# A cross-attention kernel on one core: the out projection's contraction packed into three groups of 128 rows, and the loop over batches written out

## The reference

```python
q = heads(hidden_states @ W_q)
k_t, v_t = heads(text_ehs @ W_k), heads(text_ehs @ W_v)
probs_t = softmax(einsum('bhsd,bhtd->bhst', q, k_t) * attn_scale)
text_out = einsum('bhst,bhtd->bhsd', probs_t, v_t)
k_ip, v_ip = heads(ip_ehs @ W_k_ip), heads(ip_ehs @ W_v_ip)
attn_scores = einsum('bhsd,bhnd->bhsn', q, k_ip) * attn_scale
qsem = l2norm(einsum('bhst,bte->bhse', probs_t, text_ehs))
sem = einsum('bhse,bne->bhsn', qsem, l2norm(ip_ehs))
probs_ip = softmax(attn_scores + 0.5 * sem) * spatial_mask[None, None, :, None]
ip_out = einsum('bhsn,bhnd->bhsd', probs_ip, v_ip)
out = (text_out + ip_out) @ W_out + b_out + residual
```

## Time and profile before

| | |
|---|---|
| median of 3 runs | 360.89 us (360.53 to 361.3) |
| the profiled execution: its time, its span | 363.37 us, 361.6 us |
| busy: PE, DVE, ACT, POOL | 332.5, 304.6, 299.9, 165.0 us |
| instructions: PE, DVE, ACT, POOL | 2434, 2068, 1303, 314 |
| mean granted TensorE clock | 0.995 |
| chain that ended last: PE, ACT, DVE, issue, DMA | 68%, 13%, 11%, 5%, 2% |
| moved by DMA | 16.72 MB, mean 46 GB/s |

### The profile page before, as it was taken

The page is one execution under the profiler, slowest core; times in us unless marked ns, Lnnn a source line. Parts: engine busy times, 40 slices in busy tenths (PEclk is TensorE's granted clock), DMA queues, the critical chain, the costliest instruction groups (busy, mean ns, idle before and its releaser), DMA issues.

```text
span 361.6 us, 10181 instructions
## 1 busy us (share of the span) xinstructions
PE 332.5 (92%) x2434; PEld 312.3 (86%) x2434; DVE 304.6 (84%) x2068; ACT 299.9 (83%) x1303; POOL 165.0 (46%) x314
## 2 busy tenths in 40 slices
PE   4799998889999999989999999979999999999974
PEld 4797877778999999989999999979999999999863
DVE  5557567999999999977999999979999999999963
ACT  4646699989899999977989999979999999999941
POOL 2034602636464646463464646444646464524241
PEclk9999999999999999998999999999999999999999
DMA  6940011000101010101001010101010101000001
GB/s 230 327 130 0 2 45 49 2 1 21 56 20 56 21 55 22 55 25 44 29 24 38 31 39 18 56 23 54 20 54 19 55 19 54 20 21 18 20 20 54
DMA packets 14301, 16.72 MB, mean 46 GB/s; under 512 B 1928, under 2 KB 13704, under 8 KB 14248
## 3 DMA queue, kind: packets, MB, share of 16 engines
q1 hardware_dynamic: 14248, 16.20, 14.4%
HBM read 10.13 MB, written 5.24 MB: 43 GB/s over the span
## 4 chain that ended last, share of the span: by engine, by line
PE 68%; ACT 13%; DVE 11%; issue 5%; DMA 2%; SPq 1%; ACTq 0%
PE gv_ps L936 18%; PE mi_ps L963 14%; PE mi_ps L899 11%; PE et_ps L923 9%; PE sc_ps L915 8%; ACT e_sb L554 7%; DVE place_ctxT L709 2%; DMA x_nat<-in_x 2%; DVE qs L691 2%; ACT qs L546 2%; PE mi_ps L881 2%; PE gv_ps L1054 1%; DVE negmax L701 1%; PE mi_ps L950 1%; DVE u_all L840 1%
## 5 line engine op out<-in xcount | busy, mean ns | idle before, releaser
L554 ACT ACTIVATE e_sb<-sc_ps,negmax 128x60 f32<-128x60 f32 x640 | 146.7, 315 | 15.5 <-DVE negmax L701 13.5
L936 PE MATMUL gv_ps<-tab,place_w 128*128 128x162 f32 x640 | 115.4, 302 | 3.2 <-ACT place_ctxT L563 3.0
L709 DVE CUSTOM_DVE_ANT_0 place_ctxT<-gv_ps,e_sb 128x60 f32<-128x60 f32 x640 | 99.7, 211 | 11.9 <-PE gv_ps L936 11.3
L936 PEld LDWEIGHTS gv_ps<-tab,place_w 128*128 128x128 f32 x640 | 94.7, 191 | 4.4 <-issue 4.3
L915 PE MATMUL sc_ps<-km,qs 128*128 128x256 f32 x320 | 77.5, 324 | 0.2 <-DVE qs L691 0.2
L492 POOL TENSOR_TENSOR place_w<-place_ctxT,rsum 128x320 f32<-128x320 f32 x32 | 23.8, 745 | 116.9 <-DVE rsum L819 116.9
L923 PE MATMUL et_ps<-ident,e_sb 128*128 128x128 f32 x320 | 64.5, 283 | 10.2 <-ACT e_sb L554 9.4
L701 DVE TENSOR_REDUCE negmax<-sc_ps 128x4 f32<-128x240 f32 x160 | 63.4, 396 | 0.0
L567 ACT COPY place_w<-et_ps 128x256 f32<-128x256 f32 x160 | 62.3, 389 | 0.7 <-PE et_ps L923 0.7
L923 PEld LDWEIGHTS et_ps<-ident,e_sb 128*128 128x128 f32 x320 | 39.1, 140 | 21.3 <-ACT e_sb L554 15.9
L709 DVE DVE_READ_ACCUMULATOR2_ANT quad<- 128x1 f32 x640 | 52.5, 82 | 0.0
(11 more groups left out here) (153 smaller groups left out, 587.6 us busy)
## 6 DMA issues: line engine op xcount, KB each, us to landing
x_nat<-in_x SPq DMA_DIRECT2D x16, 320.0 KB, 3.1
out<-place_w SPq DMA_DIRECT2D x32, 160.0 KB, 1.8
place_ctx<-in_ctx SPq DMA_DIRECT2D x4, 256.0 KB, 3.4
place_w<-in_L_xattn_W_v SPq DMA_DIRECT2D x1, 640.0 KB, 8.5
place_w<-in_L_xattn_W_k SPq DMA_DIRECT2D x1, 640.0 KB, 10.2
place_w<-in_L_xattn_W_k_ip SPq DMA_DIRECT2D x1, 640.0 KB, 11.7
place_w<-in_L_xattn_W_v_ip SPq DMA_DIRECT2D x1, 640.0 KB, 9.9
place_ctxT<-place_w SPq DMA_DIRECT2D x16, 40.0 KB, 1.9
```

What stands on the lines that cost most here:

```text
L554: last = nc.scalar.activation(e_sb[:, slot, TOK * j:TOK * j + T], sc_ps[:, bank, TOK * j:TOK * j + T], ACT.Exp, bias=negmax[:, slot, j:j + 1])
L709: last = v.tensor_tensor_reduce(out=junk[:, u % 2, j, 0:T], in0=gv_ps[:, u % 2, TABW * j:TABW * j + T], in1=e_sb[:, u % ERING, TOK * j:TOK ...
L936: last = mm(gv_ps[:, u % 2, 2 * TABW * r:2 * TABW * r + 2 * TABW], eT[:, u % TRING, P * r:P * r + P], tab[:, batch.parity, h:h + 2, :].rea ...
```

## The change

- The four image tokens' weights of a head sum to the mask (softmax, then times the mask). So three of them, and the mask, say as much as four: the contraction becomes 320 rows of attention + 60 rows (20 heads x 3, for the differences of v_ip to the last token's) + 1 row of the mask (for the last token's v_ip, summed over the heads) + 1 row of ones (for the bias) = 382 rows, which are padded to three groups of 128. A tile is gathered in `mixed`, transposed by three transposes and projected by nine products; the third group's right side is `u_all`, now 126 rows: the last 64 rows of W_out, 60 of u, one of the last token, the bias.
- ACT's three copies of the transposed tile become one of 384 columns, and so do DVE's three subtractions.
- Part 0 of the out projection has five products instead of six, part 1 four instead of five.
- GpSimd no longer adds the bias to x; its load and buffer are gone. `mixed` keeps four tiles.
- At the start DVE makes the differences of the image tokens (`ip_dif`, two operations) and gathers the last token's values (`vip_last`, three small copies). The five blocks of u have 96 rows, and there is a sixth of 8 rows, three products that are accumulated, with a sixth copy. PE, ACT and SP wait for six blocks. Only two thirds of W_out are split into `wo_parts`.
- SP places u by 34 transfers: 16 of 24 rows, 8 of 12 rows, 8 of one row, one that spreads the last 64 rows of W_out to all eight batches, one for the bias. ACT waits for all 34 before its first copy of u_all, in the same unit as before.
- The last tile: two transposes and six products, then one transpose and three products.
- All 8 batches are written out, with constants in the waits.

The diff, cut to that:

```diff
-        wo_parts = sb("wo_parts", [P, 2, QC, C], F32R)
-        bias_all = sb("bias_all", [P, C])
+        wo_parts = sb("wo_parts", [P, 2, 2, C], F32R)
...
-            sp.wait_ge(u_copied, 5)
+            sp.wait_ge(u_copied, 6)
+            sp.dma_start(u_nat[0:64], w_out[2 * P:C, :].unsqueeze(1).to_broadcast([64, B, C])).then_inc(u_placed, DMA)
             for b in range(B):
                 for m in range(2):
-                    r, blk = 32 * (b % 4), 2 * m + b // 4
-                    sp.dma_start(u_nat[32 * m:32 * m + 32, b], u_sb[r:r + 32, blk]).then_inc(u_placed, DMA)
-                sp.dma_start(u_nat[64:80, b], u_sb[16 * b:16 * b + 16, 4]).then_inc(u_placed, DMA)
+                    r, blk = 24 * (b % 4), 2 * m + b // 4
+                    sp.dma_start(u_nat[64 + 24 * m:88 + 24 * m, b], u_sb[r:r + 24, blk]).then_inc(u_placed, DMA)
+                sp.dma_start(u_nat[112:124, b], u_sb[12 * b:12 * b + 12, 4]).then_inc(u_placed, DMA)
+                sp.dma_start(u_nat[124:125, b], u_sb[b:b + 1, 5]).then_inc(u_placed, DMA)
+            sp.dma_start(u_nat[125:126], b_out.rearrange("(a b c) -> a b c", a=1, b=1).to_broadcast([1, B, C])).then_inc(u_placed, DMA)
...
-                    nc.scalar.copy(attnT[:, 0:2 * P], ps[:, 0:2 * P])
-                    nc.scalar.copy(attnT[0:64, 2 * P:3 * P], ps[0:64, 2 * P:3 * P])
-                    nc.scalar.copy(attnT[0:IPROWS, 3 * P:4 * P], ps[0:IPROWS, 3 * P:4 * P]).then_inc(attnT_hi, 1)
+                    nc.scalar.copy(attnT[:], mi_ps[:, misc_bank(("at", 0, index)), 0:QC * P]).then_inc(attnT_hi, 1)
...
                     if u == U_SLOT:
-                        act.wait_ge(u_placed, 3 * B * DMA)
-                    nc.scalar.copy(u_all[0:IPROWS, u - U_SLOT, 0], u_nat[0:IPROWS, u - U_SLOT]).then_inc(u_hi_made, 1)
+                        act.wait_ge(u_placed, U_PLACED * DMA)
+                    nc.scalar.copy(u_all[0:OUT_ROWS, u - U_SLOT, 0], u_nat[0:OUT_ROWS, u - U_SLOT]).then_inc(u_hi_made, 1)
...
+                v.tensor_tensor(attnT_low[:], mi_ps[:, misc_bank(("at", 0, t)), 0:QC * P], attnT[:].bitcast(F32),
+                                ALU.subtract).then_inc(attnT_lo, 1)
...
                 for c in range(QC):
-                    tr(ps[0:QROWS[c], P * c:P * c + P], attn[:, par, P * c:P * c + QROWS[c]], ident[:])
-                tr(ps[0:IPROWS, 3 * P:4 * P], pip[:, par].rearrange("p h n -> p (h n)"), ident[:]).then_inc(attnT_done, 1)
+                    last = tr(ps[:, P * c:P * c + P], mixed[:, t % ARING, P * c:P * c + P], ident[:])
+                last.then_inc(attnT_done, 1)
...
+                steps = [(high[:, P * c:P * c + P], wo_parts[:, n, c, :]) for c in range(2) for n in range(2)]
+                steps += [(low[:, P * c:P * c + P], wo_parts[:, 0, c, :]) for c in range(2)]
+                high2, low2 = high[0:OUT_ROWS, 2 * P:3 * P], low[0:OUT_ROWS, 2 * P:3 * P]
+                steps += [(high2, u_all[0:OUT_ROWS, b, 0, :]), (high2, u_all[0:OUT_ROWS, b, 1, :]),
+                          (low2, u_all[0:OUT_ROWS, b, 0, :])]
...
+            pe.wait_ge(u_copied, 3)
+            for m in range(QC):
+                last = mm(BANKS[U_BANKS[5]][0:B, 0:C], vip_last[0:QROWS[m], m, :], wo[0:QROWS[m], m, :],
+                          start=m == 0, stop=m == QC - 1)
+            last.then_inc(pre_u, 1)
+            pe.wait_ge(u_copied, 6)
...
-            with eng.Fori(0, LOOP_STEPS) as step:
-                for place in range(2):
-                    body(Batch(step=step, place=place))
...
+            for u in range(ALL_UNITS + 2 * GROUPS - 2):
```

More of the change, by code:

```diff
@@ L351, in store @@
[L351 to L363, removed]
@@ L454, in _ @@
                 pool.wait_ge(k_lo, 2 * c + 2)
-                km_step(Batch(0), c)
-            pool.wait_ge(in_bias, DMA)
+                km_step(0, c)
             pool.wait_ge(in_mask, DMA)
-            add_bias(Batch(0), 0)
-            def nxt(batch):
-                return (Batch(batch.number + 1) if batch.step is None else
-                        Batch(step=batch.step, place=batch.place + 1))
-            def builds(batch, s, part):
-                if not batch.has(1, 1, B):
+            g.tensor_copy(mixed[:, :, MASK_COL:MASK_COL + 1], mask_sb[:].unsqueeze(2)).then_inc(consts_made, 1)
@@ L528, in _ @@
+            for t in range(ALL_TILES + 2):
+                tile(t)
         @block.scalar
@@ L669, in _ @@
+            for u in range(ALL_UNITS + GROUPS + 1):
+                slot(u)
+            act.wait_ge(last_done, 1)
+            nc.scalar.copy(last_attnT[:, 0:2 * P], LAST_ATTN[:, 0:2 * P]).then_inc(last_hi, 1)
+            act.wait_ge(last_done, 2)
+            nc.scalar.copy(last_attnT[:, 2 * P:3 * P], LAST_IP).then_inc(last_hi, 1)
         @block.vector
@@ L672, in _, with x_low @@
             v.memset(tab[:], 0.0).then_inc(zeros_made, 1)
-            for place in range(YRING):
-                dve.sem_inc(y_stored[place], DMA)
-            def x_low(batch, half, n):
-                dve.wait_ge(xT_hi, batch.count(2 * HALVES, 2 * half + n + 1))
-                ps = mi_ps[:, misc_bank(batch, half - 1, "x", n), :]
+            def x_low(half, n):
+                dve.wait_ge(xT_hi, 2 * half + n + 1)
+                ps = mi_ps[:, misc_bank(("x", n, half)), :]
                 if n == 0:
@@ new lines, in add_residual, with slot @@
+            def add_residual(product, t):
+                dve.wait_ge(out_done, t + 1)
+                if t >= YRING:
+                    dve.wait_ge(y_stored[t % YRING], DMA * (t // YRING))
+                v.tensor_tensor(y_sb[:, t % YRING], product, x_nat[:, t // 2 % XRING, t % 2], ALU.add).then_inc(y_made, 1)
+            def slot(u):
+                t, j = divmod(u, GROUPS)
+                before, before2 = 0 <= t - 1 < ALL_TILES, 0 <= t - 2 < ALL_TILES
+                par, par2 = (t - 1) % 2, t % 2
+                if u + LEAD < ALL_UNITS:
+                    maxima(u + LEAD)
@@ L1133 @@
+                if not early and u < ALL_UNITS:
+                    table_products(u)
+            for u in range(ALL_UNITS + 2 * GROUPS - 2):
+                if u == ALL_UNITS + GROUPS + 1:
+                    last_attn_transposes()
+                slot(u)
+            last_products()
 _INS = ["x", "ctx_2048", "fside_S_0", "L0_xattn_W_q", "L0_xattn_W_k", "L0_xattn_W_v",
```

665 lines of the change are left out of this document (282 added, 383 removed).

## The result

The changed kernel took 351.85 us (median of 5 runs, the kernel before beside it 360.53); the ratio is 0.973, with a 95% interval of 0.970 to 0.976. In a second measurement it took 350.91 against 361.15, ratio 0.9734 (0.9705 to 0.9764). So it is 2.7% faster, 8.7 to 10.2 us. The forecast was 349.6, between 344.5 and 358.

What follows compares the result with a forecast made beforehand. PE was taken to set the pace, DVE and ACT right behind. -8.8 - 0.84 - 5.5 - 1.9 + 1.6 + 4.1 = -11.3 us took the profiled 363.4 to 352.1; less 2.5, 349.6 us, range 344.5 to 358.

Steps and rivals of the forecast that it cites:

- The steady half: Each half batch (two tiles) gets 0.63 us shorter, bounds 0.30 to 1.0; over fourteen halves -8.8 us.
- the wait of 0.18 for DVE's low halves: PE's wait before six out-projection products goes as DVE finishes 0.44 earlier, but only 0.04 of it counts.
- so PE sets the pace: In the steady half PE, 92% busy, bounds the kernel, with DVE (84%) and ACT (83%) right behind.
- Rival B: DVE and ACT take the gain: the half shrinks by 0.3 only, 354.2 us; chance 0.10.
- ACT's saving: One copy of 384 columns of the transposed tile in place of three saves ACT 0.17 us a tile.
- The loop: Written-out batches lose the stops after two jumps: 3.55 (some 1.6 of it half clock) and 1.93, sum -5.5 us.
- The 2.5: The old kernel's runs had median 360.9, 2.5 under the profiled 363.4; the same was taken off 352.1.
- The stop: In unit 10 ACT waits for SP to place u: 3.3 plus 0.8 for half clock, +4.1 us (1 to 6).
- over 6 us: Sign of being wrong: ACT's wait before its first u_all copy is over 6 us; about 3 expected.
- rival A: Small transfers placing u cost SP 0.29 more for each of 24 issues; stall grows by 7.0, 356.6 us; chance 0.14.
- DVE's 0.84 in the second half of batch 0: That half is DVE's, so two tiles' shorter subtractions count nearly whole: 2 x 0.42, -0.84 us.
- Rivals C and D: C: SP's issues queue behind the w_out load, 367.1, chance 0.07; D: straight code stalls as the loop did, 355.1, chance 0.04.

Runs made afterwards that it cites:

- exp. 2: The kernel before with only its batches (and SP's loop) written out: 356.83 us, ratio 0.9895 to the kernel before.
- exp. 6: The changed kernel with only DVE's subtraction in three pieces again: 364.06 us, ratio 1.0059 to the kernel before.
- exp. 7: The changed kernel with only ACT's copy in three pieces again: 358.81 us, ratio 0.9922 to the kernel before.
- exp. 4: The changed kernel with ACT's copy and DVE's subtraction both in three pieces again: 365.88 us, ratio 1.014 to the kernel before.
- exp. 5: The changed kernel with PE's eleven products and four transposes a tile put back, some done twice: 358.65 us, ratio 0.9918 to the kernel before.
- exp. 12: The changed kernel with U_SLOT 14, and DVE's guard and image softmax reciprocal left out: 344.85 us, ratio 0.9565 to the kernel before.
- exp. 10: The kernel before with u's transfers cut to 24 and 12 rows, number unchanged, a quarter of u's rows unplaced: 360.79 us, single execution.
- exp. 3: The changed kernel with the first unit that needs the placed u moved from 10 to 14 (U_SLOT): 345.55 us, ratio 0.9564 to the kernel before.
- exp. 8: The changed kernel with U_SLOT 14, u's sixth block made in unit 7 and its rows placed last: 344.79 us, ratio 0.9534 to the kernel before.
- exp. 11: The changed kernel with U_SLOT 14, and the guard's square made on GpSimd by plain multiplication: 344.5 us, ratio 0.9552 to the kernel before.
- exp. 9: The changed kernel with U_SLOT 14, and both reciprocals moved from DVE to GpSimd as a power of -1: 465.69 us, ratio 1.2899.

## Why the prediction was right, and where its steps were not

**The steady half.** Forecast -0.63, bounds 0.30 to 1.0. The stretches above give -0.80; over all whole halves, the two with a jump and the one behind the first left out, the mean goes from 18.63 to 17.86, -0.77. Between the marks that makes 10.7 us (16.2 less 3.9 for the jumps and 1.6 for a clock, below) where the forecast had 8.8. The bound of 17.7 to 18.35 held. The part of the chain that shrank is the out projection:

```profile
192.34 0.73 PE mi_ps L865 x5
...
194.09 0.59 PE mi_ps L865 x4
...
200.68 0.74 PE mi_ps L865 x5
...
202.53 0.59 PE mi_ps L865 x4
```

These are 2.65 a half. Before, the pieces at the same places were 0.89 and 1.07 and, between them, two of five products:

```profile
186.21 0.74 PE mi_ps L963 x5
...
196.01 0.73 PE mi_ps L963 x5
```

together 3.43. Of the 0.78 less, 0.59 are the four products, whole as forecast. The rest is the wait of 0.18 for DVE's low halves: it went whole, where I counted 0.04. This is the term that was mis-sized. The transposes, counted at nothing, gave nothing: the 0.11 that the chain no longer spends on one of them comes back at the scores two steps later.

The step "so PE sets the pace" was only half of the mechanism, and the price of 0.04 for DVE came from it. The half periods tell it:

| kernel | PE | DVE | ACT | half, us |
|---|---|---|---|---|
| before | as before | as before | as before | 18.65 |
| exp. 2 | as before | as before | as before | 18.60 |
| changed | less | less | less | 17.85 |
| exp. 6 | less | as before | less | 18.61 |
| exp. 7 | less | less | more than before | 18.29 |
| exp. 4 | less | as before | more than before | 18.68 |
| exp. 5 | as before | less | less | 18.33 |
| exp. 12 | less | still less | less | 17.87 |

Against exp. 2, which is written out like the changed kernel, PE's saving and ACT's without DVE's give nothing (exp. 6), the shorter copies without PE's saving 0.27 (exp. 5), all together 0.75. So before there were two paths of nearly the same length, and the longer, by some 0.3, was not PE's alone but the one that passes through DVE: the stretch of the chain shown in exp. 6 runs over its subtractions. Rival B saw that risk, but gave it to the wrong side: DVE did not take the gain, it made it possible. GpSimd's saving is in all these runs but exp. 2, and in exp. 6 it gives nothing either.

**ACT's saving: sized about right, and not tested.** The forecast had 0.17 a tile. The groups by line look as if it were 0.43, since the means of the three copies are 398, 271 and 274 ns and that of the one is 517:

```profile
L629 ACT CAST attnT<-mi_ps 128x256 fp32r<-128x256 f32 x31 | 12.3, 398 | 2.0 <-PE mi_ps L951 2.0
...
L631 ACT CAST attnT<-mi_ps 80x128 fp32r<-80x128 f32 x31 | 8.5, 274 | 0.0
L630 ACT CAST attnT<-mi_ps 64x128 fp32r<-64x128 f32 x31 | 8.4, 271 | 0.0
```

But these lengths overlap. In order of time, in the kernel before, each copy starts before the one ahead of it has ended:

```profile
332.58 0.37 ACT L629 CAST attnT<-mi_ps 128x256 fp32r<-128x256 f32 x1
...
332.85 0.26 ACT L630 CAST attnT<-mi_ps 64x128 fp32r<-64x128 f32 x1
...
333.01 0.27 ACT L631 CAST attnT<-mi_ps 80x128 fp32r<-80x128 f32 x1
```

The three take 0.70 from first start to last end and the one takes 0.52: 0.18 less. In exp. 7 the third piece lies in other rows (64 to 127), and it starts only when the second has ended, as does the operation behind it:

```profile
147.44 0.40 ACT L549 CAST attnT<-mi_ps 128x256 fp32r<-128x256 f32 x1
147.70 0.30 ACT L550 CAST attnT<-mi_ps 64x128 fp32r<-64x128 f32 x1
148.01 0.26 ACT L551 CAST attnT<-mi_ps 64x128 fp32r<-64x128 f32 x1
148.36 0.92 ACT L473 ACTIVATE e_sb<-sc_ps,negmax 128x60 f32<-128x60 f32 x4
```

From the first start to the start of the next operation, where ACT didn't wait, the medians are 0.58 before, 0.37 in the changed kernel and 0.84 in exp. 7. So exps. 4 and 7 put 0.47 a tile on ACT where the change had taken 0.21 off. Exp. 7's 0.44 a half is the price of that, and an upper bound for ACT's own saving; what this is worth alone isn't shown. Why the pieces of exp. 7 don't overlap stays open. On DVE the pieces of exp. 6 cost what they did before (0.95 and 0.94, by the same measure). DVE's forecast was exact, 0.55 for 384 columns against 0.553.

**The loop.** Forecast -5.5; exp. 2 measured -3.8, and exp. 10's two stretches with a jump give (20.61 - 18.65) + (20.58 - 18.65) = 3.9. The other 1.6 was the half clock after the first jump, which that profiled execution had and exp. 10's had not. The 2.5 by which the profiled execution was above the median can be taken apart with exp. 10, which has the loop and ran at the median (360.79). The profiled one had this 1.6 more, and a start 1.6 longer, where the first x arrived late; exp. 10 had a slower end, by 0.7. The chains at the same place of the start, before and in exp. 10:

```profile
3.57 7.17 DMA x_nat<-in_x
...
39.74 1.95 PE mi_ps L1034 x12
```

```profile
38.16 1.96 PE mi_ps L1034 x12
```

I let the change take the clock's 1.6 away and then took it off once more inside the 2.5. That step failed: without it the forecast would have been 351.2, between the two measured medians (350.91 and 351.85). The late start was rightly taken off.

**The end.** Forecast -1.9, measured 14.98 - 16.97 = -2.0.

**The start and the stop.** The block's products take 1.82 on the chain where I had 1.6. The stop costs 5.4 (exp. 3) against a forecast of 4.1 with bounds of 1 to 6. ACT's wait in it is 6.2 where I had 3.8, and "over 6 us" was one of my own signs of being wrong: it came true, though the time stayed in the range. Sized too small were two terms. SP's 34 issues took from 46.06 to 70.73, 24.7 us or 0.73 each, where I had 22.1 and 0.65: rival A's mechanism was there at less than half its price, some 0.12 instead of 0.29 for each of the 24, or 2.9 us. Exp. 10 shows it in the old kernel by the number of rows alone. The rule of the Trainium skill ("DMA: Bandwidth & Descriptors", on why a DMA increments its semaphore by 16) agrees with these rows: 24 and 12 rows divide over 12 engines, not 16, and the sequencer that issues has the missing increments to write. The eight issues of a single row were cheaper (0.54 to 0.56), which took back some 0.4. And the clock fell to 0.50 for 3.9 us, as after the first jump and not as after the second, so the full price was due and not half of it. The Trainium skill's statement ("TensorE: Matmul & The Clock Gate", Part 1), that an idle PE falls to half clock, agrees with this stop; in exp. 10 PE was idle for about 1.8 us at each jump, in two pieces, and the clock stayed at 1.00. ACT came to the wait at 66.1 and not 67.2, since x had arrived 1.4 earlier in this execution: both sides of the wait moved with it. ACT's 1.1 earlier and the landing's 1.2 later (72.2 for 71.05) make up the 2.4 by which I had the wait too short.

**The sum, by the experiments:** -10.7 (half) - 3.9 (jumps) - 2.0 (end) + 1.8 (block) + 5.4 (stop) = -9.4 us, against -10.2 between the medians of the second measurement and -8.7 in the first. DVE's 0.84 in the second half of batch 0 can't be read out: the stop lies in that stretch. The forecast of -11.3 was 1.9 too much: -8.8 was too small by 1.9, but -5.5 too large by 1.6, the stop too cheap by 1.3, the block by 0.2, and 0.84 wasn't found. That it came so near is in part luck, since the errors go both ways. Rivals C and D are ruled out: none of the 34 issues took more than 0.84, and no stop appears in the written-out batches.

**A better version.** Experiments 3, 8, 11 and 12 all lie between 344.5 and 345.6. Of the changed kernel's time 5.4 us is to be had by one number (exp. 3). The rest of the half is PE's, plus the 1.7 us of the chain just shown, in which ACT makes the queries' high halves and the exponentials: less DVE work is worth nothing there, which exp. 12 shows. Less ACT work was not tried.

## What to carry to other kernels

Where three engines are busy for 92, 84 and 83% of a span, a cut on the busiest alone may give nothing: undo each part of a saving alone and read the half period, since the engine that has most of the chain isn't the only one that sets it. Check in order of time that what an experiment puts back costs what it cost before: the mean lengths of a group overlap on ACT and don't add up. Before a stall is priced, look whether the execution in which it was read had a clock dip that the median hasn't. When a block of work is added ahead of a wait, move the first user of its result as well: here four units were worth 5.4 us.

## What was not expected of the hardware

- GpSimd's power costs 3.55 us for 128x20 fp32 elements, against 0.27 for DVE's reciprocal of the same tile, while its plain multiplication of the same size takes 0.23 (exp. 11).
- An issue on SP took longer for fewer rows: 0.71 us for 12 rows against 0.59 for 16 (exp. 10). It isn't so for every number: the single row took 0.54 (the chain of the changed kernel).
- Three copies on ACT overlap in the kernel before (0.70 us for all); with the third in rows 64 to 127 it and the next operation wait for the one ahead (exp. 7, 0.82 us and then a gap).
- Some profiled executions end at half clock and some don't. In the last slices of the page exps. 2, 3, 4, 6, 7, 8, 9 and 10 show a dip; the kernel before, the changed one and exps. 5, 11 and 12 show none. In exp. 2 eleven products took 2.93 there instead of 1.85, about 1 us. What decides it stays open. The last 15 us of exp. 3, and under them those of exp. 12:

```profile
330.00:345.40 15.40, 9.16 (x39) 7.41 (x37) 5.76 (x32) 2.94 (x11) 3.44 (x10) 0.76 0.12 43
```

```profile
327.00:342.20 15.20, 8.94 (x57) 7.47 (x55) 7.29 (x47) 4.19 (x17) 5.33 (x14) 1.00 0.13 44
```

The granted clock is 0.76 and 1.00. Busy time on PE is nearly equal, but for 39 matmul instructions in the one and 57 in the other.
